# Two layers of a graph-attention kernel: two sets of sums and the keys' terms by DMA in layer 2, a two-piece f32r spread of them in layer 3

## The chip, the cores and the metric

One core of one Trainium2 chip runs the whole program. The metric is the device time of one execution in microseconds; lower is better. The engines are named as the profile names them: PE (matrix multiply; PEld its weight loads), DVE (vector), ACT (activations), POOL (GpSimd), and SP, whose queue issues nearly all DMAs.

## The reference

Four graph-attention layers run one after the other on 8 graphs of 1024 nodes and 128 features, each followed by a residual and a layer norm. Layers 0 and 1 are dot-product attention with four heads. Layers 2 and 3, which the change touches, score additively:

```python
# layer 2, one head of width 128            # layer 3, four heads of width 32
s_i = Wh @ a1                               # ei, ej per head
s_j = Wh @ a2
e = leaky_relu(s_i[:, :, None] + s_j[:, None, :], negative_slope=0.2)
e = where(mask, e, -inf)                    # layer 3: -9e15
attention = softmax(e, axis=-1)
h_prime = attention @ Wh                    # then elu
```

Here s_j is the "keys' term": one number per node j. To take the softmax stably, the kernel needs for each node i the largest s_j among its neighbours.

## The kernel before, in words

A **unit** is one graph and head: 8 units in layer 2, 32 in layer 3. A unit is worked in 16 **tiles** of 128 keys by 512 queries, numbered tt = 0 to 15: tiles 0 to 7 are the first half of the queries (c = 0), 8 to 15 the second (c = 1). A tile passes through the engines so:

- `scores` (PE, L1046 or L1051, then L1053): mask and query terms summed in one of four PSUM banks (0 to 3). For two tiles in four ACT has first written a relu there (L832).
- `settle` (DVE, L1382, the other two tiles in four) and `exps` (ACT, L858): the exponential.
- `take_low` (POOL, L329): reads two operands in SBUF and writes the low part of the f32 exponential as f16.
- `weigh` (PE, L1094): 20 matmuls of 129 columns (33 in layer 3) that add the tile into the sums, 6 tiles after its scores (`LAGS`).

After the last tile of a half DVE divides the sums (`half_done`, L1431 to L1437) and adds one to `s_accfree`. In layer 2 the sums of a half fill banks 6 and 7, and both halves use the same two; `weigh` at the first tile of a half waits on `s_accfree` until the half before is divided. In layer 3 a half needs one bank, and the two halves alternate between 6 and 7.

The largest neighbour is found ahead of time. `spread` (PE, L1003) multiplies a column of ones by the row of s_j, in plain f32 with one row, so that all 128 partitions of banks 4 and 5 hold the row. `take_max` (DVE, L1350, a custom instruction that adds the mask and takes the maximum) then runs 8 times per unit, over that PSUM row and `mask_n` in SBUF. Of unit U+2's maxima six are taken during unit U, after tiles 7, 9, 11, 13, 14 and 15 (`MAX_AFTER`), and the last two during unit U+1, after tiles 1 and 2 (`MAX_NEXT`). `spread` for unit U+2 is issued after the scores of tile 7 (`SPREAD_AT`). `find_shift` (DVE, L1330 to L1334) follows at tile 4, then SP's `place_shift` puts the result, in 8 small DMAs (L527), into the row that `scores` of the next unit reads.

All of it is written as one instruction stream per engine; every engine runs its stream in order and stops at each semaphore wait. SP's stream in each unit is `store_output`, `place_shift`, a wait for PE, `load_unit` for three units ahead (L494). Before the first tile of a layer, DVE takes all maxima of unit 0, finds its shift, and takes six of unit 1.

## Time and profile before

| what | us |
|---|---|
| median of 3 runs | 2969.57 (2963.59 to 2971.39) |
| the profiled execution | 2962.04 |
| its span | 2960.2 |
| layer 2, first scores to last `weigh` | 1729 to 2026 |
| layer 3, first `spread` to last `weigh` | 2184 to 2882 |

Over the span PE is busy 78%, DVE 73%, POOL 63%, ACT 54%. An engine's idle time is given in the profile with what ended it ("<-"); an engine that waits on a semaphore at the head of its queue is idle. "PEclk" is the granted TensorE clock as a share of 2.4 GHz; 0.50 is 1.2 GHz.

### The profile page before, as it was taken

The numbers are of one execution on the slowest core, as the hardware profiler recorded it, in microseconds if no ns is written. First come the engines' busy times: TensorE is split into PE (matmuls) and PEld (weight loads), VectorE is DVE, ScalarE is ACT, GpSimd is POOL, SyncE is SP. The second block draws the span as 40 slices with busy tenths as digits, with TensorE's granted clock in tenths as the row PEclk, the third lists the DMA queues.
The fourth block names the chain that finished last, engine by engine and source line by source line (L and its number), as shares of the span: only waits on it lengthen the run. The fifth ranks groups of instructions, "written<-read, shape, count | busy, mean of one in ns | idle before, by whom it ended". The sixth has DMA issues, their size and how long they took to land.

```text
span 2960.2 us, 89198 instructions
## 1 busy us (share of the span) xinstructions
PE 2309.2 (78%) x32745; PEld 1617.6 (55%) x33080; DVE 2157.0 (73%) x4078; ACT 1585.4 (54%) x2273; POOL 1853.8 (63%) x1837
## 2 busy tenths in 40 slices
PE   4588888887565999999957668884659988989980
PEld 3366666666442556666635446663426665666660
DVE  4499999999464999999933354433759988888965
ACT  3344444454363555555534534444727776777775
POOL 2288888888341778777853434443318877777873
PEclk9788888888676999999976679997769998898995
DMA  7922333331575222232235421102631211111117
GB/s 245 322 69 71 77 78 78 77 77 27 127 229 172 61 63 61 63 71 64 63 77 168 136 73 52 52 16 95 156 83 50 48 45 42 46 44 42 50 31 162
DMA packets 336189, 263.48 MB, mean 89 GB/s; under 512 B 229688, under 2 KB 293432, under 8 KB 335856
## 3 DMA queue, kind: packets, MB, share of 16 engines
q1 hardware_dynamic: 331248, 241.83, 30.7%
q0 software_dynamic: 4608, 16.78, 1.5%
q8 instruction: 262, 4.29, 0.6%
q14 instruction: 71, 0.58, 0.1%
HBM read 162.84 MB, written 95.36 MB: 87 GB/s over the span
## 4 chain that ended last, share of the span: by engine, by line
PE 45%; issue 17%; DVE 16%; ACT 7%; SPq 5%; DMA 4%; POOL 2%; DVEq 1%; ACTq 0%; POOLq 0%
PE ps L1094 15%; PE ps L1053 7%; DVE xn L1408 4%; SPq L527 4%; PE ps L1034 3%; PE ps L1003 3%; PE ps L941 3%; ACT xn L721 2%; DVE cv L1370 2%; DVE full L1350 2%; DMA qs<-nshift 2%; PE ps L1012 2%; PE ps L1038 2%; PE ps L965 2%; PE ps L1051 2%
## 5 line engine op out<-in xcount | busy, mean ns | idle before, releaser
L329 POOL TENSOR_TENSOR xc<-part 128x512 f16<-128x512 f32 x1536 | 1604.7, 1073 | 626.6 <-ACT part L858 473.1
L1094 PE MATMUL ps<-vs,part 128*128 128x33 bf16 (+1 forms) x13824 | 845.9, 188 | 46.2 <-DVEq L1443 44.5
L1094 PEld LDWEIGHTS ps<-vs,part 128*128 128x128 bf16 x13824 | 674.0, 101 | 352.9 <-issue 207.6
L1350 DVE CUSTOM_DVE_ANT_0 full<-ps,mask_n 128x1024 bf16<-128x1024 f32 x576 | 695.5, 1218 | 150.7 <-PE ps L1003 71.8
L1094 PE MATMUL ps<-vs,xc 128*128 128x33 bf16 (+1 forms) x9216 | 775.5, 186 | 9.5 <-issue 9.5
L1094 PEld LDWEIGHTS ps<-vs,xc 128*128 128x128 f16 x9216 | 593.9, 99 | 6.8 <-issue 6.8
L840 ACT ACTIVATE part<-cv,lift 128x1024 f32<-128x1024 f32 x256 | 294.8, 1152 | 321.5 <-DVE cv L1370 298.5
L858 ACT ACTIVATE part<-ps 128x512 f32<-128x512 f32 x512 | 305.6, 597 | 281.3 <-PE ps L1038 281.3
L1053 PE MATMUL ps<-qs,sel 128*128 128x512 f32 x640 | 416.0, 651 | 17.0 <-ACT ps L832 17.0
L1034 PE MATMUL ps<-qs,ks 128*128 128x512 f32 x512 | 287.9, 565 | 123.3 <-DVE cv L1370 91.4
L1382 DVE SCALAR_TENSOR_TENSOR cv<-ks,colx,ps 128x512 f32<-128x512 f32 x320 | 238.7, 746 | 182.9 <-PE ps L1053 145.9
L858 ACT ACTIVATE part<-cv,cols 128x512 f32<-128x512 f32 x320 | 229.7, 718 | 239.4 <-DVE cv L1382 233.3
L1370 DVE SCALAR_TENSOR_TENSOR cv<-ps,mask_t 128x1024 f32<-128x1024 f32 x256 | 311.8, 1219 | 43.9 <-PE ps L1034 20.3
L1038 PE MATMUL ps<-qs,ks 97*128 97x512 f32 x512 | 301.8, 590 | 3.1 <-DMA qs<-nshift 3.0
L858 ACT ACTIVATE part<-ps,colx 128x512 f32<-128x512 f32 x320 | 215.0, 672 | 81.0 <-PE ps L1053 75.9
L1076 PEld LDWEIGHTS ps<-vs,part 128*128 128x128 bf16 x2048 | 160.9, 98 | 133.2 <-issue 95.5
L1076 PE MATMUL ps<-vs,part 128*128 128x99 bf16 x2048 | 229.6, 212 | 1.0 <-POOL xc L329 1.0
L832 ACT ACTIVATE ps<-ks,colx 128x512 f32<-128x512 f32 x316 | 218.7, 692 | 11.4
L1078 PE MATMUL ps<-vs,xc 128*128 128x66 bf16 x2048 | 216.0, 194 | 0.0
L1012 PE MATMUL ps<-ks,qs 96*128 96x512 f32 x512 | 188.4, 451 | 21.1 <-DMA vs<-v_d 18.6
L1034 PEld LDWEIGHTS ps<-qs,ks 128*128 128x128 f32 x512 | 111.0, 218 | 132.5 <-DVE cv L1370 90.9
L1078 PEld LDWEIGHTS ps<-vs,xc 128*128 128x128 f16 x2048 | 168.6, 99 | 0.0
(145 smaller groups left out, 3313.7 us busy)
## 6 DMA issues: line engine op xcount, KB each, us to landing
qs<-q_d SPq DMA_DIRECT2D x224, 128.0 KB
ks<-k_d SPq DMA_DIRECT2D x224, 128.0 KB
ks<-row_d SPq DMA_DIRECT2D x40, 512.0 KB
vs<-v_d SPq DMA_DIRECT2D x96, 198.0 KB
q_d<-part SPq DMA_DIRECT2D x32, 512.0 KB
k_d<-part SPq DMA_DIRECT2D x32, 512.0 KB
ctx_d<-xn SPq DMA_DIRECT2D x96, 128.0 KB, 1.8
xc<-ctx_d SPq DMA_DIRECT2D x96, 128.0 KB, 4.4
```

Of the source, the lines that this page charges most:

```text
L329: eng.tensor_tensor(plo[:, r, :], prob[:, r, :], phi[:, r, :], ALU.subtract).then_inc(low_done(layer, u, s)[0], 1)
L840: act.activation(prob[:, r:r + 2, :], arg[:, a:a + 2, :], ACT.Exp, scale=2.0 * CLIP, bias=lift[:, 0:1]).then_inc(s_exp, 2)
L858: act.activation(prob[:, r, :], src, ACT.Exp, **more).then_inc(s_exp, 1)
L1012: mm = pe.matmul(ps[:, at + c, :], qs[0:96, n, k * P:(k + 1) * P], ks[0:96, n, c * HALF:(c + 1) * HALF], start=True, stop=True)
L1034: mm = pe.matmul(bank, ks[:, n, blk_j], qs[:, n, cut], start=True, stop=True)
L1038: mm = pe.matmul(bank, ks[0:97, n, blk_j], qs[0:97, n, cut], start=False, stop=True)
L1053: mm = pe.matmul(bank, sel[:, 2, :], qs[:, n, cut], start=False, stop=True, skip_group_check=True)
L1076: pe.matmul(ps[:, 6 + c, at_a:at_a + V3], phi[:, r, it * P:(it + 1) * P], vs[:, n, at_v:at_v + V3], start=opens, stop=False, skip_group_ch ...
L1078: mm = pe.matmul(ps[:, 6 + c, at_a:at_a + 66], plo[:, r, it * P:(it + 1) * P], vs[:, n, at_v:at_v + 66], start=False, stop=True, skip_grou ...
L1094: mm = pe.matmul(acc, half[:, r, it * P:(it + 1) * P], vs[:, n, at:at + width], start=opens and h == 0 and v == 0, stop=h == 1 and v == 1, ...
L1350: dve.tensor_tensor_reduce(junks[k % 2], src, mask_n[:, k, :], 1.0, least, ALU.add, ALU.max, accum_out=dst).then_inc(s_nmax, 1)
L1370: dve.scalar_tensor_tensor(arg[:, a:a + 2, :], ps[:, r:r + 2, :], -0.5, mask_t[:, j:j + 2, c * HALF:(c + 1) * HALF], ALU.max, ALU.min).the ...
```

## The change

In layer 2 the second half of the queries sums in banks 4 and 5, the first in 6 and 7, and `weigh` waits for the half before the last one. The keys' terms no longer pass through PE and PSUM there: SP copies the row of s_j from HBM to all 128 partitions of SBUF (`load_keys`, 512 KB), in turn into half of `full` and into `work`, and `take_max` reads it there. In layer 3 `spread` stays, but takes 0.2 s_j as two f32r pieces in two rows and multiplies by ones divided by 0.2; the second row costs one more load per unit. The two scratch rows of `take_max` now share one half of `full`.

```diff
-LOADS = (9, 7, 7, 8)
+LOADS = (9, 7, 6, 9)
-        junks = [full[:, k, :].bitcast(BF16)[:, 0:NODES] for k in range(2)]
+        junks = [full[:, 0, :].bitcast(BF16)[:, k * NODES:(k + 1) * NODES] for k in range(2)]
+        keys = [full[:, 1, :], work[:, :, :].rearrange("p t f -> p (t f)")]
...
-                    go(qs[32:33, n, :].bitcast(F32), row_d[0, bass.ds(r + heads, 1)])
+                    if layer == 3:
+                        for k in range(2):
+                            go(qs[32 + k:33 + k, n, :].bitcast(F32), row_d[2 + k, bass.ds(r + heads, 1)])
...
+            def load_keys(g, n):
+                sp.wait_ge(s_nmax, max_count(SHIFT0[2] + g - 1))
+                sp.dma_start(keys[n % 2], row_d[0, bass.ds(g * 8 + 1, 1)].to_broadcast([P, NODES])
+                             ).then_inc(s_keys[n % 2], 16)
...
+                if layer == 2:
+                    for n in range(2):
+                        load_keys(n, n)
...
+                        if layer == 2 and not (last and n >= UNROLL - 2):
+                            load_keys(g + 2, n)
...
-                        mm = pe.matmul(ps[:, 4 + c, :], sel[32:33, 1, :].bitcast(F32),
-                                       qs[32:33, n, c * HALF:(c + 1) * HALF].bitcast(F32), start=True, stop=True)
+                        mm = pe.matmul(ps[:, 4 + c, :], sel[32:34, 1, :], qs[32:34, n, c * HALF:(c + 1) * HALF],
+                                       start=True, stop=True)
...
-                            pe.wait_ge(s_accfree, H - (0 if layer == 2 else 1) - 2 * UNITS[0])
+                            pe.wait_ge(s_accfree, H - 1 - 2 * UNITS[0])
...
-                                acc = ps[:, 6 + it // 2, it % 2 * width:(it % 2 + 1) * width]
+                                acc = ps[:, 6 - 2 * c + it // 2, it % 2 * width:(it % 2 + 1) * width]
...
-                            if layer > 1 and one_after and tt == SPREAD_AT:
+                            if layer == 3 and one_after and tt == SPREAD_AT:
...
-            dve.memset(sel[32:34, 1, :].bitcast(F32), 1.0).then_inc(s_sel, 1)
+            dve.memset(sel[32:34, 1, :].bitcast(F32), 1.0 / SLOPE).then_inc(s_sel, 1)
...
+                        if layer == 2:
+                            src = keys[n % 2]
+                        if k == 0 and layer == 2:
+                            dve.wait_ge(s_keys[n % 2], u * (16 * (UNROLL // 2)) + (n // 2 + 1) * 16)
...
-                        banks = ((6, 2), (7, 2)) if layer == 2 else ((6 + c, IB),)
+                        banks = ((6 - 2 * c, 2), (7 - 2 * c, 2)) if layer == 2 else ((6 + c, IB),)
```

On PE, at tile 7 of layer 2's first unit (L1046 and L1053 are scores, L1003 the spread, L1094 `weigh`), before:

```order
L1046 MATMUL ps<-mask_t,ident_b 128x512 [waits s_relu]
L1053 MATMUL ps<-qs,sel 128x512
L1003 MATMUL ps<-qs,sel 128x512 [waits s_nmax,s_stk2]
L1003 MATMUL ps<-qs,sel 128x512
L1094 MATMUL ps<-vs,part 128x129 [waits s_lo]
L1094 MATMUL ps<-vs,part 128x129 x2
L1094 MATMUL ps<-vs,xc 128x129 x2
```

and in the changed kernel, where the same functions have other line numbers (L1063 and L1070 scores, L1111 `weigh`):

```order
L1063 MATMUL ps<-mask_t,ident_b 128x512 [waits s_relu]
L1070 MATMUL ps<-qs,sel 128x512
L1111 MATMUL ps<-vs,part 128x129 [waits s_lo]
L1111 MATMUL ps<-vs,part 128x129 x2
L1111 MATMUL ps<-vs,xc 128x129 x2
```

The spread and its two waits are gone from between scores and `weigh`. On DVE, from the end of `find_shift` at tile 4 to tile 9 of a layer 2 unit ("ISA full,top" is `take_max`, "ISA top" the read of its result), before:

```order
L1334 SCALAR_TENSOR_TENSOR colx<-cols 128x8
L1382 SCALAR_TENSOR_TENSOR cv<-ks,colx,ps 128x512 [waits s_exp,s_score,s_colx]
L1350 ISA full,top<-ps,mask_n 128x1024 [waits s_nmax,s_nsc]
L1350 ISA top 128x1
L1382 SCALAR_TENSOR_TENSOR cv<-ks,colx,ps 128x512 [waits s_exp,s_score]
L1350 ISA full,top<-ps,mask_n 128x1024 [waits s_nmax]
```

and now:

```order
L1350 SCALAR_TENSOR_TENSOR colx<-cols 128x8
L1402 SCALAR_TENSOR_TENSOR cv<-ks,colx,ps 128x512 [waits s_exp,s_score,s_colx]
L1370 ISA full,top<-full,mask_n 128x1024 [waits s_nmax,s_keys0]
L1370 ISA top 128x1
L1402 SCALAR_TENSOR_TENSOR cv<-ks,colx,ps 128x512 [waits s_exp,s_score]
L1370 ISA full,top<-full,mask_n 128x1024 [waits s_nmax]
```

The order is the same; the first operand of `take_max` moves from PSUM (ps) to SBUF (full, in the next unit work), and the wait from PE's s_nsc to the DMA's s_keys0. On SP's queue, the third unit's loads and what follows ahead of layer 2's first tile, before:

```order
L494 DMA qs<-row_d 1x1024
L494 DMA ks<-row_d 128x1024
L494 DMA qs<-row_d 1x1024 x2
L494 DMA cols<-col_d 128x8 x2
L494 DMA vs<-v2_d 128x3096
L527 DMA qs<-nshift 1x128x1 [waits s_shcol]
L527 DMA qs<-nshift 1x128x1 x7
```

and now:

```order
L497 DMA ks<-row_d 128x1024
L497 DMA qs<-row_d 1x1024 x2
L497 DMA cols<-col_d 128x8 x2
L497 DMA vs<-v2_d 128x3096
L539 DMA full<-row_d 128x1024 [waits s_nmax]
L539 DMA work<-row_d 128x1024 [waits s_nmax]
L533 DMA qs<-nshift 1x128x1 [waits s_shcol]
L533 DMA qs<-nshift 1x128x1 x7
```

The first two key rows are queued behind the loads of three units.

## Rows read from the trace of the kernel before

**Rows 1.** Windows: length, busy us (instructions) by engine, PEclk, DMA share, GB/s

```profile
1808.20:1845.70 37.50, 31.32 (x355) 25.00 (x358) 18.58 (x41) 16.79 (x25) 16.38 (x16) 0.91 0.17 51
...
2402.10:2421.60 19.50, 18.41 (x378) 12.81 (x383) 18.05 (x36) 15.53 (x25) 16.09 (x17) 1.00 0.20 49
2334.80:2354.90 20.10, 19.30 (x376) 13.21 (x382) 18.31 (x35) 15.55 (x25) 16.12 (x17) 0.92 0.21 48
2354.90:2380.70 25.80, 20.79 (x351) 13.59 (x357) 18.42 (x36) 15.96 (x26) 17.22 (x17) 0.74 0.16 39
```

**Rows 2.** Waits, layer 2 (1730 to 2030): who waited for whom, total, times, longest

```profile
PE ps L1094 <- DVEq L1443: 44.5, 15, 3.6
```

**Rows 3.** Timeline of PE in layer 2: start, length, instruction, [idle before]

```profile
1813.07 0.51 PE L1094 MATMUL ps<-vs,part 128*128 128x129 bf16 x3 [2.55 <-DVEq L1443]
...
1815.28 0.99 PE L1053 MATMUL ps<-qs,sel 128*128 128x512 f32 x1
1816.20 2.01 PE L1003 MATMUL ps<-qs,sel 1*128 1x512 f32 x4
1818.14 0.35 PE L1094 MATMUL ps<-vs,part 128*128 128x129 bf16 x3
...
1819.34 0.58 PE L1053 MATMUL ps<-qs,sel 128*128 128x512 f32 x1
1819.77 0.35 PE L1094 MATMUL ps<-vs,part 128*128 128x129 bf16 x3
...
1820.97 0.58 PE L1053 MATMUL ps<-qs,sel 128*128 128x512 f32 x1
```

**Rows 4.** Groups by line, layer 2: count, busy us, mean ns, idle before

```profile
L329 POOL TENSOR_TENSOR xc<-part 128x512 f16<-128x512 f32 x128 | 131.0, 1040 | 189.6 <-ACT part L858 153.6 <-issue 36.0
...
L1350 DVE CUSTOM_DVE_ANT_0 full<-ps,mask_n 128x1024 bf16<-128x1024 f32 x54 | 65.6, 1219 | 31.4 <-PE ps L1003 29.6 <-DVE xn L1437 1.8
L1382 DVE SCALAR_TENSOR_TENSOR cv<-ks,colx,ps 128x512 f32<-128x512 f32 x64 | 47.8, 747 | 114.7 <-PE ps L1053 94.0 <-issue 20.5
```

**Rows 5.** Timeline of POOL and DVE in layer 1's node stage

```profile
801.08 2.33 POOL L640 TENSOR_TENSOR vs<-xc,rows 128x1024 f32<-128x1024 f32 x1
...
802.06 2.44 DVE L1251 TENSOR_TENSOR full<-full,rows 128x1024 f32<-128x1024 f32 x1 [3.44 <-ACT full L721]
```

**Rows 6.** DVE lines with all operands in SBUF: ns min/median/max

```profile
L1251 DVE TENSOR_TENSOR full<-full,rows x8: 1224/2439/2446, 767.4 to 900.9; 128x1024 f32<-128x1024 f32 x8
```

```profile
L329 DVE TENSOR_TENSOR xc<-part x128: 685/1015/1573, 968.5 to 1516.0; 128x512 f16<-128x512 f32 x128
```

```profile
L1331 DVE SCALAR_TENSOR_TENSOR nshift<-shift x40: 166/961/966, 1722.6 to 2849.1; 128x8 f32<-128x8 f32 x40
```

**Rows 7.** Timeline ahead of layer 2's first tile

```profile
1709.02 3.75 PE L1003 MATMUL ps<-qs,sel 1*128 1x512 f32 x4 [16.56 <-DMA vs<-v_d]
...
1713.08 1.23 DVE L1350 CUSTOM_DVE_ANT_0 full<-ps,mask_n 128x1024 bf16<-128x1024 f32 x1 [17.58 <-PE ps L1003]
...
1726.51 1.22 DVE L1350 CUSTOM_DVE_ANT_0 full<-ps,mask_n 128x1024 bf16<-128x1024 f32 x1 [3.56 <-PE ps L1003]
```

**Rows 8.** One window there, columns as in Rows 1

```profile
1714.00:1716.00 2.00, 0.00 (x0) 0.00 (x0) 2.00 (x5) 0.00 (x0) 0.00 (x0) 0.50 0.46 186
```

**Rows 9.** Timeline of PE in layer 3

```profile
2403.06 1.98 PE L1003 MATMUL ps<-qs,sel 1*128 1x512 f32 x4
2404.97 0.24 PE L1094 MATMUL ps<-vs,part 128*128 128x33 bf16 x3
```

**Rows 10.** Windows of 1 us in layer 3, columns as in Rows 1

```profile
2340.00:2341.00 1.00, 1.00 (x22) 0.83 (x22) 1.00 (x4) 0.09 (x1) 0.69 (x1) 0.50 0.17 17
```

**Rows 11.** Waits, layer 3 (2230 to 2882)

```profile
DVE cv L1382 <- PE ps L1053: 50.4, 49, 3.2
```

**Rows 12.** Timeline ahead of layer 3's first tile

```profile
2201.48 1.22 DVE L1350 CUSTOM_DVE_ANT_0 full<-ps,mask_n 128x1024 bf16<-128x1024 f32 x1 [3.55 <-PE ps L1003]
```

**Rows 13.** Window in layer 2's node stage, columns as in Rows 1

```profile
1600.00:1660.00 60.00, 46.96 (x237) 35.31 (x235) 23.00 (x69) 32.61 (x52) 28.76 (x40) 0.68 0.63 190
```

More of the change, by code:

```diff
@@ L223, in build @@
         s_relu = sem("s_relu")
+        s_keys = [sem("s_keys0"), sem("s_keys1")]
         s_open = sem("s_open")
@@ L1131, in heads @@
                         unit_ready(n, 0)
-                        if layer > 1:
+                        if layer == 3:
                             spread(n, U + n)
-                            continue
-                        for k in range(BLOCKS if n == 0 else len(MAX_AFTER[1])):
+                        for k in range((BLOCKS if n == 0 else len(MAX_AFTER[1])) if layer == 1 else 0):
                             top_scores(n, k, U + n)
@@ L1336, in find_shift, with take_max @@
                     dve.wait_ge(s_colx, U - SHIFT0[2] + 1)
-                def take_max(k, U, n):
+                def take_max(k, U, n, u=0):
                     dve.wait_ge(s_nmax, max_count(U) + k - 1)
@@ L1346, in take_max @@
                         src, least, dst = pf[:, 4 * HALF:6 * HALF], LOWEST, top[:, k, 0:1]
-                        if k == 0:
-                            dve.wait_ge(s_nsc, BLOCKS * SHIFT0[2] + U - SHIFT0[2] + 1)
+                        if layer == 2:
+                            src = keys[n % 2]
+                        if k == 0 and layer == 2:
+                            dve.wait_ge(s_keys[n % 2], u * (16 * (UNROLL // 2)) + (n // 2 + 1) * 16)
+                        elif k == 0:
+                            dve.wait_ge(s_nsc, BLOCKS * SHIFT0[2] + U - SHIFT0[3] + 1)
                     dve.sem_inc(s_carry, 1)
@@ L1461, in body @@
                             if tt in MAX_NEXT[layer] and next_one:
-                                take_max(MAX_NEXT[layer][tt], U + 1, n + 1)
+                                take_max(MAX_NEXT[layer][tt], U + 1, n + 1, u)
                             if layer > 1 and tt == FIND_AT and next_one:
@@ L1465, in body @@
                             if tt in MAX_AFTER[layer] and one_after:
-                                take_max(MAX_AFTER[layer][tt], U + 2, n + 2)
+                                take_max(MAX_AFTER[layer][tt], U + 2, n + 2, u)
                         e = s - lag - 1
```

## The prediction, made before the changed kernel ran

> **What bounds the kernel now.** I read the windows of one unit in each layer first, then the waits of layer 2, then the timelines of PE and DVE where the waits stood. A layer 2 unit takes 37.5 us. PE is busy for 31.3 of them, DVE for 18.6, ACT for 16.8, POOL for 16.4 [rows 1]: PE sets the pace there and is itself stopped for some 6 us. In 15 places `weigh` waits for DVE to divide the half before, 44.5 us in all [rows 2]. The timeline shows one: 2.55 us idle at 1813.07, and after it the score matmul at 1815.28 takes 0.99 us instead of 0.58, because the granted clock stands at its lower level, 1.2 GHz, until PE has worked a while. Then comes the spread, from 1816.20 to 1818.14, 1.94 us; and then tiles that follow each other by 1820.97 - 1819.34 = 1.63 us [rows 3].
>
> Layer 3 is another case. A unit whose clock stays at 2.4 GHz takes 19.5 us, with PE busy 18.4 and DVE 18.05; one with a stretch at 1.2 GHz takes 20.1 [rows 1]. In the first kind DVE is the bound: its 1.4 idle microseconds are short gaps between its own dependent instructions. So PE time there is worth less than its length.
>
> **The change, part by part.** The sum is made against the profiled execution, 2962.04 us (span 2960.2); the median of the runs is 2969.57, 7.5 above it.
>
> *Two sets of sums.* The wait for the half before becomes a wait for the one before that, which DVE divided 8 tiles (13 us) earlier. All 44.5 us of idle go [rows 2]. So does what they cost in clock: of the 37.5 us of a unit, 16 tiles of 1.63 are 26.1, two stops (44.5/15 each) 5.9, the spread 1.9; the 3.6 left over are two restarts at the lower clock, 1.8 each, 15 of them 27 us.
>
> *No spread in layer 2.* Six spreads lie between tiles (units 2 to 7), 6 x 1.94 = 11.6 us of PE [rows 3]. Together 83 us, if nothing else takes PE's place; a unit would then take 26.1 us.
>
> *Maxima from SBUF.* This is the price. Before, `take_max` reads one operand from PSUM and takes 1219 ns at any time [rows 4]. Now both lie in SBUF, and POOL's `take_low`, 16 a unit of 1040 ns [rows 4], also reads SBUF. What that does is seen elsewhere in the trace. In layer 1's node stage POOL's L640 runs from 801.08 to 803.41; DVE's L1251, both operands in SBUF, starts at 802.06 and ends at 804.50, which is POOL's end plus 1.1 us [rows 5]. Alone it takes 1224 ns, beside POOL 2439; L329 on DVE 685 alone, 1015 in the middle, 1573 at most; even the 8-element L1331 goes from 166 to 961 [rows 6]. So a DVE instruction with two SBUF operands waits for POOL's current one to end, up to 1.04 us, and POOL waits for it in turn. The Trainium skill says the same (SBUF — State Buffer, "Who interferes with whom": two SBUF inputs on DVE contend with a GpSimd instruction that reads SBUF, and the loser is blocked for the whole instruction). By that rule, the trace agrees, and it speaks against this part of the change.
>
> How much: POOL's 16 x 1.04 = 16.6 and DVE's 8 x 1.22 = 9.8 come to 26.4 us of exclusive use in a unit that PE wants to do in 26.1. If every max waits a full `take_low`, DVE needs 18.6 + 8 x 1.04 = 26.9, and some 1.6 more for two slowed instructions of `find_shift`: 28.5 us, 2.4 above PE, 19 us over 8 units. If no max waits, nothing. The 6 tiles between scores and `weigh` (9.8 us, against about 3.1 for one tile's way through settle, exp and low) absorb much, but five maxima fall on tiles 13 to 18, where DVE falls behind. I take 1.5 us a unit, nearer the upper end, 12 us.
>
> *Start of layer 2.* Before, DVE's first max is at 1713.08, after a spread of 3.75 us at the lower clock that began when unit 0's loads were there; later DVE stands 3.56 us until the second spread is done [rows 7]. Now the first key row is queued behind three units' loads, of which the last arrive about 1715: in 1714 to 1716 the DMA engines are busy 0.46 of the time at 186 GB/s, so 404 GB/s when they work [rows 8]. 0.5 MB at that rate are 1.3 us more, and with about a microsecond to land it is there near 1717. That is 4 us later, and 3.6 come back because unit 1's maxima no longer wait. I book nothing; if the rows land together with the very last load it is 3 to 5 us worse. The wait of `load_keys` on SP is for maxima taken long ago, and the copy is issued about a unit ahead of its use, so nothing behind it on SP's queue (`store_output`, `place_shift`) is held up; the 4 MB in total lie in a queue that is busy 17% of a unit [rows 1].
>
> Layer 2: 83 - 12 = 71 us.
>
> *The f32r spread in layer 3.* Before, four passes and 1.91 us (2403.06 to 2404.97) [rows 9]. The scores of a tile are also two matmuls of 512 columns, one bf16 and one f32r; from their start, 1819.34, to the next `weigh`, 1819.77, pass 0.43 us [rows 3]. So I take 0.43 for the two f32r matmuls of the new spread, and 0.87 at 1.2 GHz. No row shows one with two rows. PE saves 1.5 us a unit. With DVE as the bound only these parts count:
> - Ahead of the first tile both spreads lie on the chain, at 3.75 us each (the row in [rows 7] is layer 2's, layer 3's two are as long, and the second again holds DVE for 3.55 [rows 12]): 2 x 2.9 = 5.8 us.
> - Nineteen units of 20.1 us hold about 3.4 us at 1.2 GHz (a microsecond of it is in [rows 10]), in which PE loses 1.7 us. With 1.5 us less work PE no longer holds DVE up, and the unit goes to DVE's 19.4 to 19.5: 19 x 0.65 = 12 us. DVE's waits for PE's scores, 50.4 us in the layer [rows 11], bound this and the next item from above.
> - Eight units go slower for other reasons (five of about 26 us, in which PE stands still for 5 us where the loop turns, [rows 1] has one, and three of 21 to 22 behind it). There PE leads, mostly at the lower clock, and I take 1.1 us each, 9 us.
>
> Layer 3: 27 us. Its extra load of 4 KB a unit on SP lies behind `place_shift` and costs nothing; if SP were late it would show as PE waiting for nshift.
>
> **Sum:** 2962.0 - 71 - 27 = 2864. The runs lie somewhat above the profiled one; I forecast 2867.
>
> **The rivals.**
> *A, the forecast:* PE stays the bound of layer 2 at 27 to 28 us a unit, DVE of layer 3.
> *B, the port between DVE and POOL decides layer 2:* in the dense stretch settle, exp and low come so late that PE stops again and restarts at 1.2 GHz. For it: 26.4 us of exclusive use in 26.1. Against it: 9.8 us of slack per tile, and ACT is free a third of the time. At 33 us a unit, which is 28.5 and two stops with restart of 2.2 each, layer 2 gains 83 - 8 x 6.9 = 28 us: 2910.
> *C, PE's saving counts in full in layer 3:* 30 x 1.5 + 5.8 = 51 us there instead of 27, and 2840. Against it: DVE's 18.05 busy microseconds with their gaps make the 19.5 that the fast units take now [rows 1].
> *D, slower: the clock in layer 3.* PE gets 2.5 to 3 idle us a unit, and the level falls when it idles: in the node stage ahead of layer 2 PE is busy 78% of the time and the mean clock is 0.68 [rows 13]. PE needs 18.4 - 1.5 = 16.9 us a unit at full clock; at a mean of 0.87 it would match DVE, and to eat layer 2's 71 us over 32 units the unit must reach 20.2 + 2.2 = 22.4 us, a mean clock of 0.75. Worked out at 0.72, 23.5 us a unit: 2891 + 32 x 3.3 = 2997. Against it: a PE that is waited for does not idle, so the loss limits itself.
> *E, no change:* only if PE's waits were replaced one for one, say by the key rows landing late for every unit. They are asked for a unit ahead.
>
> **How the numbers follow.** A 0.68, B 0.18, C 0.08, D 0.03, E 0.03. A's own range is from 2848 (no lock cost, and layer 3 with 31) to 2885 (lock cost 19, layer 3 only 17, start 5 worse, then the runs' scatter). To leave out 2 in 10 at most, the range runs to B: 2842 to 2910. A measurement here tells from no change what is over 0.3% (9 us). Faster 0.94, same 0.02, slower 0.04.
>
> **What would show it.** Layer 2: no PE wait on `half_done`, units of 27 to 28 us, clock near 1.0 within them, 8 maxima a unit with a median between 1.3 and 2.2 us, and POOL's `take_low` with a tail above 1.04. Layer 3: spread 0.43 us, units near 19.5, DVE hardly ever waiting for scores. The first max of layer 2 near 1717 on the old scale. I am wrong if the maxima stay at 1.22 (then 2855), if layer 2 units exceed 30 us (B), or if layer 3 units stay at 20.1 in spite of the shorter spread, which would mean that the lower clock, not the spread, sets them.

## The result, and the profile after

| what | before | changed | forecast |
|---|---|---|---|
| median, us | 2970.48 (2963.59 to 2991.56, 4 runs) | 2841.65 (2835.98 to 2847.84, 4 runs) | 2867 |
| span of the profiled execution | 2960.2 | 2834.1 | 2862 |
| layer 2, first to last `take_low` | 283.6 | 200.3 | 283.6 - 71 = 212.6 |
| layer 3, first to last `take_low` | 668.3 | 626.9 | 668.3 - 21 = 647.3 |

The ratio is 0.9555, 95% interval 0.9503 to 0.9607: 129 us faster where 103 were forecast. The time lies 0.35 us below the range (2842 to 2910) and 6 below the forecast's own (2848 to 2885). In the profiled executions layer 2 gave 12 us more than was forecast and layer 3 gave 20 us more. Ahead of them the changed kernel is 3.5 us later (last `take_low` of layer 1 at 1519.9, before 1516.4); from there to layer 2's first tile nothing changed (219.0 us, before 218.6), as booked.

The spans of the two layers are read from POOL's instructions: duration in ns (min/median/max), then first and last start. Before:

```profile
L329 POOL TENSOR_TENSOR xc<-part x128: 1038/1040/1050, 1735.0 to 2018.6; 128x512 f16<-128x512 f32 x128
L329 POOL TENSOR_TENSOR xc<-part x512: 1036/1040/1070, 2209.9 to 2878.2; 128x512 f16<-128x512 f32 x171
```

and in the changed kernel, with the maxima of layer 2 (L1370):

```profile
L332 POOL TENSOR_TENSOR xc<-part x128: 1034/1042/2114, 1738.9 to 1939.2; 128x512 f16<-128x512 f32 x128
L332 POOL TENSOR_TENSOR xc<-part x512: 1032/1042/1073, 2126.1 to 2753.0; 128x512 f16<-128x512 f32 x171
L1370 DVE CUSTOM_DVE_ANT_0 full<-work,mask_n x25: 1211/1389/1953, 1739.7 to 1892.7; 128x1024 bf16<-128x1024 f32 x25
L1370 DVE CUSTOM_DVE_ANT_0 full<-full,mask_n x24: 1212/1390/2086, 1744.8 to 1867.0; 128x1024 bf16<-128x1024 f32 x24
```

The contention is there: maxima of up to 2.09 us instead of 1.22 [rows 4], `take_low` of up to 2.11. The windows (columns as in [rows 1]: length, PE, PEld, DVE, ACT, POOL, PEclk, DMA share, GB/s) show what became of it. One unit of layer 2, then of layer 3 an ordinary unit, one at the loop's turn, the one behind it, and the first:

```profile
1817.30:1844.10 26.80, 26.80 (x363) 22.45 (x361) 22.46 (x42) 17.06 (x26) 21.35 (x18) 1.00 0.29 91
...
2306.80:2326.40 19.60, 17.59 (x384) 12.65 (x384) 18.11 (x37) 15.63 (x26) 16.22 (x17) 1.00 0.21 49
2425.80:2448.90 23.10, 18.51 (x370) 12.94 (x370) 18.62 (x36) 16.14 (x26) 17.11 (x17) 0.85 0.16 43
2448.90:2467.40 18.50, 17.92 (x396) 12.90 (x393) 16.41 (x35) 15.03 (x24) 15.18 (x16) 1.00 0.21 52
2129.20:2147.10 17.90, 16.80 (x359) 12.03 (x360) 17.43 (x33) 15.43 (x25) 16.07 (x17) 1.00 0.21 47
```

In layer 2 PE is busy for the whole unit at 2.4 GHz, where it was busy for 31.3 of 37.5 us at a mean clock of 0.91 [rows 1]; DVE's busy time went from 18.6 to 22.5 us and POOL's from 16.4 to 21.4, both still below 26.8. The six units between start and end of the layer take 23.9 to 26.8 us, 25.7 in the mean. No PE wait on the divided half is left (it was [rows 2]); DVE's wait for scores in layer 3 halved, from [rows 11] to:

```profile
DVE cv L1402 <- PE ps L1070: 26.5, 26, 2.9
```

The new spread on PE in layer 3, to be compared with the old one in [rows 9]:

```profile
2307.31 0.58 PE L1070 MATMUL ps<-qs,sel 128*128 128x512 f32 x1
2307.82 0.73 PE L1020 MATMUL ps<-qs,sel 2*128 2x512 f32 x2
2308.48 0.24 PE L1111 MATMUL ps<-vs,part 128*128 128x33 bf16 x3
```

From its start to the next `weigh` pass 0.66 us, before 1.91. The saving is 1.25 us; the forecast was a spread of 0.43 us and a saving of 1.5.

The units of layer 3, in us (means), as the 30 periods from unit 1's to unit 31's between the starts of the second instruction of `find_shift` (L1331 before, L1347 now). Counted from its first instruction, a unit at a turn is 0.3 to 0.6 us shorter and the one behind it 0.4 to 0.7 longer; their sum stays.

| | first | 19 ordinary | 5 at a turn | 5 behind a turn |
|---|---|---|---|---|
| before | 22.5 | 19.95 | 26.1 | 20.8 |
| changed | 17.9 | 19.4 | 22.8 | 19.0 |
| gain in sum | 4.6 | 11 | 16.5 | 9 |

The ordinary units did what was forecast (12 us). The other eleven gave 30 us; 9 were booked for them. The experiments had two questions: why does the contention in layer 2 cost nothing, and where do the 30 us come from.

### The profile page after: what moved, and what is told of

It reads as the page before. It is cut to its first block, busy times and chain, and to the rows that moved or that the text cites. A ratio compares the mean times of both kernels' runs of the same rounds, so it can differ in the third digit from the quotient of the medians.

```text
span 2834.1 us, 89438 instructions
## 1 busy us (share of the span) xinstructions
PE 2200.2 (78%) x32984; PEld 1571.2 (55%) x32984; DVE 2176.8 (77%) x4078; ACT 1577.9 (56%) x2273; POOL 1882.5 (66%) x1837
## 4 chain that ended last, share of the span: by engine, by line
PE 37%; issue 18%; DVE 18%; ACT 8%; SPq 7%; DMA 5%; POOL 2%; DVEq 1%; ACTq 0%; POOLq 0%
PE ps L1111 12%; SPq L533 5%; DVE xn L1428 4%; PE ps L1070 4%; DMA qs<-nshift 3%; PE ps L958 3%; ACT xn L738 3%; DVE full L1370 3%; DVE cv L1390 2%; PE ps L1051 2%; PE ps L1063 2%; PE ps L1068 2%; PE ps L1029 2%; PE ps L982 2%; PE ps L1054 2%
## 5 line engine op out<-in xcount | busy, mean ns | idle before, releaser
L332 POOL TENSOR_TENSOR xc<-part 128x512 f16<-128x512 f32 x1536 | 1633.0, 1094 | 473.6 <-ACT part L875 326.3
L1111 PE MATMUL ps<-vs,part 128*128 128x33 bf16 (+1 forms) x13824 | 823.5, 186 | 1.2 <-DVE work L1419 1.1
L1111 PEld LDWEIGHTS ps<-vs,part 128*128 128x128 bf16 x13824 | 658.5, 99 | 272.0 <-issue 202.7
L1111 PE MATMUL ps<-vs,xc 128*128 128x33 bf16 (+1 forms) x9216 | 762.1, 184 | 4.4 <-issue 4.4
L1370 DVE CUSTOM_DVE_ANT_0 full<-ps,mask_n 128x1024 bf16<-128x1024 f32 x512 | 618.4, 1218 | 88.5 <-DVE xn L1462 29.0
L1111 PEld LDWEIGHTS ps<-vs,xc 128*128 128x128 f16 x9216 | 583.2, 97 | 0.1
L1070 PE MATMUL ps<-qs,sel 128*128 128x512 f32 x640 | 380.1, 596 | 0.0
L1093 PEld LDWEIGHTS ps<-vs,part 128*128 128x128 bf16 x2048 | 161.0, 98 | 133.1 <-issue 96.3
L849 ACT ACTIVATE ps<-ks,colx 128x512 f32<-128x512 f32 x316 | 218.7, 692 | 11.5
L1054 PE MATMUL ps<-mask_t,ident_b 128*128 128x512 bf16 x512 | 198.2, 387 | 16.2 <-DMA qs<-nshift 10.4
L1029 PE MATMUL ps<-ks,qs 96*128 96x512 f32 x512 | 188.5, 451 | 21.7 <-DMA vs<-v_d 19.2
```

The costliest lines, as they stand in the source:

```text
L332: eng.tensor_tensor(plo[:, r, :], prob[:, r, :], phi[:, r, :], ALU.subtract).then_inc(low_done(layer, u, s)[0], 1)
L1029: mm = pe.matmul(ps[:, at + c, :], qs[0:96, n, k * P:(k + 1) * P], ks[0:96, n, c * HALF:(c + 1) * HALF], start=True, stop=True)
L1054: pe.matmul(bank, ident_b[:, :], mask_t[:, j, cut], start=True, stop=False)
L1070: mm = pe.matmul(bank, sel[:, 2, :], qs[:, n, cut], start=False, stop=True, skip_group_check=True)
L1093: pe.matmul(ps[:, 6 + c, at_a:at_a + V3], phi[:, r, it * P:(it + 1) * P], vs[:, n, at_v:at_v + V3], start=opens, stop=False, skip_group_ch ...
L1111: mm = pe.matmul(acc, half[:, r, it * P:(it + 1) * P], vs[:, n, at:at + width], start=opens and h == 0 and v == 0, stop=h == 1 and v == 1, ...
```

## The experiments

Each kernel is compared with the kernel before on the same chip; "layer 3" below is the time between its first and last `take_low`.

### The parts alone

e1 is the kernel before with the f32r spread in layer 3 only:

```diff
-LOADS = (9, 7, 7, 8)
+LOADS = (9, 7, 7, 9)
...
+                        if layer == 3:
+                            mm = pe.matmul(ps[:, 4 + c, :], sel[32:34, 0, :], qs[32:34, n, c * HALF:(c + 1) * HALF],
+                                           start=True, stop=True)
+                            continue
...
+            dve.memset(sel[32:34, 0, :].bitcast(F32), 1.0 / SLOPE).then_inc(s_sel, 1)
```

> Layer 3's two-piece spread alone, layer 2 as before. Theory 1 (the parts add): layer 3 takes what it takes in the changed kernel, from first to last take_low 627 us against 668 before, plus 4 us ahead of it; the whole kernel is 45 us faster than before, about 2925 against 2970. Theory 2 (layer 3 was helped by what layer 2 left behind, such as where loads land): less than 30 us. My prediction's sum said 27 us.

Measured: 2926.65 us, ratio 0.9875 (0.9853 to 0.9897), 37 us faster. Layer 3 takes 635.6 us, 32.7 less, and layer 2 283.6 as before. An ordinary unit:

```profile
2390.20:2409.70 19.50, 17.49 (x381) 12.54 (x381) 18.05 (x35) 15.53 (x25) 16.11 (x17) 1.00 0.19 50
```

e2 is the changed kernel with the old spread in layer 3:

```diff
-LOADS = (9, 7, 6, 9)
+LOADS = (9, 7, 6, 8)
...
-                        mm = pe.matmul(ps[:, 4 + c, :], sel[32:34, 1, :], qs[32:34, n, c * HALF:(c + 1) * HALF],
-                                       start=True, stop=True)
+                        mm = pe.matmul(ps[:, 4 + c, :], sel[32:33, 1, :].bitcast(F32),
+                                       qs[32:33, n, c * HALF:(c + 1) * HALF].bitcast(F32), start=True, stop=True)
...
-            dve.memset(sel[32:34, 1, :].bitcast(F32), 1.0 / SLOPE).then_inc(s_sel, 1)
+            dve.memset(sel[32:34, 1, :].bitcast(F32), 1.0).then_inc(s_sel, 1)
```

> Layer 2's part alone, layer 3 with the plain f32 spread. Theory 1 (the parts add): layer 2 takes 200 us from first to last take_low against 284 before, layer 3 668 as before, whole kernel about 83 us faster, 2887. Theory 2: layer 3 gets shorter than 660 without any change of its own.

Measured: 2877.83 us, ratio 0.9715 (0.9692 to 0.9737), 86 us faster. The parts add up, 37 + 86 = 123 of 129 us. Against e2 the changed kernel saves 35.4 us between layer 3's first and last tile (662.3 to 626.9): first unit 4.2, 19 ordinary ones 12, five at a turn 11.5 (25.1 to 22.8 each), five behind 8 (20.6 to 19.0). So the spread is most of what works at the turn. Layer 2's part gives layer 3 another 6 to 9 us though it changes nothing in layer 3's own code: 668.3 to 662.3 without the new spread (e2 against the kernel before), 635.6 to 626.9 with it (the changed kernel against e1), most of it at the turns.

e3 keeps the keys' DMA but gives layer 2 back its single set of sums:

```diff
-                            pe.wait_ge(s_accfree, H - 1 - 2 * UNITS[0])
+                            pe.wait_ge(s_accfree, H - (0 if layer == 2 else 1) - 2 * UNITS[0])
...
-                                acc = ps[:, 6 - 2 * c + it // 2, it % 2 * width:(it % 2 + 1) * width]
+                                acc = ps[:, 6 + it // 2, it % 2 * width:(it % 2 + 1) * width]
...
-                        banks = ((6 - 2 * c, 2), (7 - 2 * c, 2)) if layer == 2 else ((6 + c, IB),)
+                        banks = ((6, 2), (7, 2)) if layer == 2 else ((6 + c, IB),)
```

> The changed kernel with one set of sums in layer 2, as before; the keys still come by DMA and are read in SBUF. Theory 1 (the stops on half_done are most of layer 2's gain, 44.5 us of idle and 27 us at the lower clock): layer 2 is about 70 us longer than in the changed kernel, 270 us from first to last take_low, and PE waits for half_done 15 times again, about 45 us. Theory 2 (the spread's removal did more than its 12 us): layer 2 below 255 us.

Measured: 2910.6 us, ratio 0.9821 (0.9801 to 0.9841). Layer 2 takes 272.4 us: the missing spread gives 11.2, which is the 11.6 forecast for it, and the second set of sums 72.1 (272.4 to 200.3), which is 44.5 + 27 = 71.5. The waits are back as they were [rows 2]:

```profile
PE ps L1111 <- DVEq L1463: 44.9, 15, 4.1
```

### The contention in layer 2

e8 replaces POOL's `take_low` in layer 2 by a memset, which reads nothing; the low part is left out of layer 2's sums.

```diff
+            if layer == 2:
+                eng.memset(plo[:, r, :], 0.0).then_inc(low_done(layer, u, s)[0], 1)
+                return
```

> The changed kernel with POOL's take_low of layer 2 replaced by a memset of the same tile: the low part of the exponential is left out and POOL reads nothing there. If the lock between DVE's two SBUF operands and POOL's reads is what lengthens layer 2's maxima (1286 ns in the middle, 2086 at most), all become 1.22 us. If layer 2 is bound by PE, its time stays within 3 us of the changed kernel's 200; if the lock still costs what I booked (12 us), it drops by that.

Measured: 2844.73 us, one run. The maxima are back at 1.22 us, every one:

```profile
L1373 DVE CUSTOM_DVE_ANT_0 full<-work,mask_n x30: 1216/1218/1228, 1739.6 to 1899.2; 128x1024 bf16<-128x1024 f32 x30
...
1798.40:1824.50 26.10, 26.10 (x352) 21.99 (x355) 18.39 (x43) 16.49 (x25) 8.38 (x16) 1.00 0.29 93
```

DVE is busy for 18.4 us again and POOL for 8.4, yet PE still fills the unit, with 16 tiles of 1.63 us. The six units from the second shift to the eighth take 153.4 us, in the changed kernel 154.0, and the layer 200.1 against 200.3. The contention is real and costs under 1 us in the whole layer, not 12.

### The two rows at the head of layer 2

e9 queues each of the two first key rows ahead of the loads of its own unit:

```diff
+                    if layer == 2 and n < 2:
+                        load_keys(n, n)
                     load_unit(layer, 0, n)
```

> The changed kernel with each of the first two key rows loaded ahead of its unit's other loads. In the changed kernel the first max of layer 2 stands at 1719.9 us, 7 us later than before. If the queue behind three units' loads is the cause, the first max starts about 10 us earlier and the whole kernel is 6 to 10 us faster than the changed one, near 2833. If other loads of unit 0 are what DVE waits for, under 3 us.

Measured: 2832.25 us, ratio 0.9553 (0.9532 to 0.9573); by the ratios, which scatter by several us, it can't be told from the changed kernel's 0.9555. The traces can tell them apart. The first max starts 191.9 us after layer 1's last `take_low`; in the changed kernel it is 200.0, before 196.7. In the changed kernel this is the wait and what the DMA engines do just ahead of it, busy all the time at 411 GB/s:

```profile
1719.93 1.23 DVE L1370 CUSTOM_DVE_ANT_0 full<-full,mask_n 128x1024 bf16<-128x1024 f32 x1 [21.89 <-DMA full<-row_d]
...
1717.00:1719.00 2.00, 0.00 (x0) 0.00 (x0) 0.00 (x0) 0.00 (x0) 0.00 (x0) 0.50 1.00 411
```

From layer 1's last `take_low` to layer 2's first pass 210.8 us, in the changed kernel 219.0; in e12 and e13, which have the same edit, 212.4 and 212.3, and in all eleven kernels with the key rows queued last 218.2 to 220.6. The place in the queue costs 8 us, and undoing it gives them.

### What bounds an ordinary unit of layer 3

e6 takes layer 3's maxima over the first 512 keys only, which takes work from DVE and none from PE:

```diff
+                    w = HALF if layer == 3 else NODES
```

> The changed kernel with layer 3's maxima taken over the first 512 keys alone (the other 512 are left out of the maximum), which takes about 4.3 us of DVE time off each unit. If DVE is the bound of layer 3 now, its units go from 19.5 us to PE's 17.6 or a little below; if PE is, they stay at 19.5.

Measured: 2794.41 us, one run; layer 3 590.6. An ordinary unit goes to 18.0 us in the mean, and PE nearly fills it. One of them:

```profile
2307.10:2324.90 17.80, 17.65 (x403) 13.02 (x405) 14.48 (x35) 15.51 (x25) 16.02 (x17) 1.00 0.22 54
```

So DVE was the bound at 19.4 us. A unit at a turn still takes 22.6 us, with a stop of PE of 3.5 to 4.4 us.

### The lower clock

e4 and e5 make the spread of the changed kernel a little longer than the old one, with seven more matmuls of 512 columns ahead of each of the 32 spreads. In e4 they are two-row f32r ones like the spread, in e5 bf16 ones over all 128 rows. At the full clock the padded spread then takes 2.28 us (median 2.29 in e4, 2.28 in e5) up to the next `weigh`, the old one 1.91.

```diff
+                    for k in range(7):
+                        pe.matmul(ps[:, 4, :], sel[32:34, 1, :], qs[32:34, n, 0:HALF], start=True, stop=True)
```

```diff
+                    for k in range(7):
+                        pe.matmul(ps[:, 4, :], ident_b[:, :], mask_t[:, 0, 0:HALF], start=True, stop=True)
```

> The changed kernel with 7 idle f32r matmuls of two rows ahead of each spread of layer 3, so that a spread costs PE about 1.9 us again, as in plain f32. Theory 1 (layer 3's gain is PE time where PE leads): layer 3 goes back to about 668 us from first to last take_low, 40 more than the changed kernel. Theory 2 (the plain f32 form itself did the harm, by other means than its length): it stays near 627.

> The same with 7 bf16 matmuls of 128 rows as the padding, also about 1.5 us. Theory 1 (PE time alone): the same layer 3 time as with the two-row padding, within 5 us, and the same stretches at 1.2 GHz. Theory 3 (the granted clock fell because of what PE did in the spread, one row, not because of its length): the stretches at 1.2 GHz inside the units are gone, units take 19.4 to 19.6 us, layer 3 is 15 us or more shorter than with the two-row padding.

Measured: e4 2901.57 us, ratio 0.9764 (0.9718 to 0.9811); e5 2870.11, ratio 0.9665 (0.962 to 0.9709). An ordinary unit, one at a turn and the one behind it, in e4:

```profile
2351.50:2371.90 20.40, 19.63 (x382) 14.12 (x386) 18.28 (x35) 15.75 (x25) 16.18 (x17) 0.92 0.19 47
2371.90:2399.60 27.70, 21.18 (x377) 14.76 (x382) 19.04 (x35) 16.69 (x26) 17.27 (x17) 0.75 0.15 36
2399.60:2420.70 21.10, 20.36 (x393) 14.55 (x396) 16.72 (x37) 15.17 (x25) 15.35 (x16) 0.92 0.19 46
```

and in e5:

```profile
2333.10:2352.60 19.50, 17.77 (x368) 12.46 (x373) 18.10 (x36) 15.64 (x26) 16.18 (x17) 1.00 0.21 49
2352.60:2379.80 27.20, 20.86 (x370) 13.84 (x373) 18.36 (x35) 15.95 (x26) 17.09 (x17) 0.81 0.15 37
2379.80:2400.40 20.60, 19.86 (x418) 14.03 (x423) 16.54 (x36) 15.61 (x25) 15.23 (x16) 1.00 0.20 48
```

Both give PE the same number of matmuls of the same columns, for the same time. With two-row f32r ones the granted clock falls to the lower level in every unit (mean 0.917 in ordinary ones, which take 20.5 us); with full-row bf16 ones it stays at 1.00 in 18 of the 19 and the unit at DVE's 19.5. Layer 3 takes 682.0 us in e4 and 654.6 in e5: 27 us are the clock alone. The two paddings differ in rows and in type, and no run separates these; that f32r alone does not do it is argued from the changed kernel, whose scores are f32r over 128 rows and whose ordinary units are all at 1.00. But e5 is still 27.7 us above the changed kernel, and nearly all of it is in the first unit (1.7), at the turns (26.6 against 22.8 us) and behind them (20.0 against 19.0).

### The turn: load traffic

At the turn SP issues the loads of a unit just as PE stops. e10 puts them off by twelve tiles in the changed kernel, e11 in the kernel before:

```diff
-                            sp.wait_ge(s_av, CREDIT + TILES * UNIT0[layer] + g * TILES)
+                            late = TILES - 4 if layer == 3 and n == UNROLL - 1 else 0
+                            sp.wait_ge(s_av, CREDIT + TILES * UNIT0[layer] + g * TILES + late)
```

> The changed kernel; in layer 3 the fourth unit's loads of each loop body are held back until PE has done two tiles of the next body, so that no load runs while PE turns the loop. In the kernels so far PE stands 3.3 to 3.6 us at the turn where the copy of 512 KB is issued 0.1 to 0.6 us before PE gets there, and 4 to 5 us, mostly with a second stop of 1.1 to 1.4, where it is issued 1 to 2 us before. Theory A (PE's stop at the turn is made longer by load traffic that is in flight): all five stops get shorter than 3.3 us and alike, layer 3 shrinks by up to 10 us. Theory B (the stop is PE's own and its length comes from what PE did before): they stay at 3.3 to 3.6 and the time stays.

> The same deferral in the kernel before, nothing else. Theory A: the five stops of 3.6 to 5.0 us and the five second ones of 1.1 to 1.7 fall to what the deferred changed kernel has, the five long units go from 26 to about 22 us, layer 3 from 668 to about 650. Theory B: they stay at 26, and the time at 2965 to 2970.

Measured: e10 2841.58 us, ratio 0.9563 (0.9517 to 0.961), layer 3 624.4; e11 2962.39, ratio 0.9983 (0.9962 to 1.0004), layer 3 662.0. The profiled execution of e10 is the fastest of its four by 10 us, so its 624.4 says little; PE's stops in it are 3.2 to 3.5 us (changed kernel 3.3 to 5.0). In e11 the first stop shrinks to 3.3 to 3.75 us from 3.6 to 5.0, but the second one, in `weigh` some 3 us later, grows from 1.1 to 1.7 us to 1.6 to 1.9, and the two together only go from 5.5 to 5.3 us in the mean:

```profile
2461.98 0.39 PE L1052 MATMUL ps<-mask_t,ident_b 128*128 128x512 bf16 x1 [3.75 <-issue]
2464.54 0.22 PE L1095 MATMUL ps<-vs,xc 128*128 128x33 bf16 x2 [1.56 <-issue]
```

The traffic explains up to 1.5 us of a first stop, and not the difference between the kernels.

### The turn: instructions, time or place

The idle time before these matmuls waits on no semaphore ("issue"). Seven padding matmuls change PE's time and the number of its instructions at once. e14 and e15 add two and seven matmuls of 33 columns ahead of each of the 32 spreads, 64 and 224 in all (the first expectation below counts e14's too high). Two bring the number of matmuls that the trace records to that of the old spread, which counts as four [rows 9]. This is e15; e14 has `range(2)`:

```diff
+                    for k in range(7):
+                        pe.matmul(ps[:, 4, 0:33], ident_b[:, :], mask_t[:, 0, 0:33], start=True, stop=True)
```

e16 runs 28 of them once, ahead of layer 3's loop, which moves only the place of the loop's body in PE's program. Theory F says that the number of instructions in the body makes the stop long, theory T that PE's time does, and the third that the body's place does.

> The changed kernel with two small full-row bf16 matmuls of 33 columns ahead of each spread, in layer 3 only (64 spreads, 128 matmuls). They add instructions to PE's loop body and next to no time. Open is why PE stops at layer 3's loop turn for 3.3 to 3.6 us in the changed kernel and for 3.6 to 5.0 us, and then once more for 1.1 to 1.7 us, in the kernel before (and 4.2 to 5.2 and 1.1 to 1.4 in the two kernels with seven padding matmuls for each spread). Theory F, the stop grows with the number of instructions in the loop's body: it becomes longer than 3.6 us or its second part comes back, the five units at a turn go from 22.8 to 24 us or more, and layer 3 from 627 to some 635. Theory T, the stop follows from PE's time, as how far PE is ahead of or behind the other engines when it comes to the turn: stops of 3.3 to 3.6 us with no second part, turn units of 22 to 23.5 us, layer 3 within 3 us of 627.

> The changed kernel with seven small full-row bf16 matmuls of 33 columns ahead of each spread, in layer 3 only: as many instructions as the kernel with seven 512-column ones, but less than a fifth of their time. Theory F, number of instructions: stops as there, 4.8 to 5.2 us and then 1.1 to 1.4, turn units near 26.5 us, units behind a turn near 20, layer 3 near 650. Theory T, PE's time: stops of 3.3 to 3.6 us with no second part, turn units of 22 to 24 us, layer 3 under 635.

> The changed kernel with 28 small matmuls of 33 columns run once, ahead of layer 3's loop: the loop's body keeps its length and only its place in PE's program moves. Theory F and theory T both: stops of 3.3 to 3.6 us, layer 3 within 3 us of 627. A third theory, that the stop depends on where the body lies in the program and not on its length: stops change here, to over 4 us or with a second part.

Measured: e14 2840.03 us, ratio 0.9558 (0.9529 to 0.9587); e15 2852.79, 0.9601 (0.9573 to 0.9629); e16 2839.64, 0.9556 (0.9519 to 0.9594). The mean units, PE's stops at the turn and, in the last column, how many 16 KB packets the DMA queue "instruction" (q8) moves between two turns:

| kernel | layer 3 | at a turn | behind | ordinary | first stop | second stop | q8 |
|---|---|---|---|---|---|---|---|
| before | 668.3 | 26.1 | 20.8 | 19.95 | 3.6 to 5.0 | 1.1 to 1.7 | 15 |
| e2, old spread | 662.3 | 25.1 | 20.6 | 20.0 | 4.4 to 6.0 | none | 15 |
| e11, deferral | 662.0 | 24.9 | 21.1 | 19.9 | 3.3 to 3.75 | 1.6 to 1.9 | 15 |
| e4, seven of 2x512 | 682.0 | 27.2 | 20.9 | 20.5 | 4.2 to 5.1 | 1.1 to 1.4 | 15 |
| e5, seven of 128x512 | 654.6 | 26.6 | 20.0 | 19.5 | 4.75 to 5.2 | 1.1 to 1.4 | 15 |
| e15, seven of 128x33 | 639.6 | 25.0 | 18.7 | 19.5 | 3.3 to 4.8 | 1.1 to 2.4 | 15 |
| e1, old layer 2 | 635.6 | 23.8 | 19.2 | 19.4 | 3.4 to 4.75 | 1.1, at two turns | 14 |
| e16, place | 634.0 | 23.8 | 19.4 | 19.4 | 3.8 to 5.1 | none | 14 |
| e14, two of 128x33 | 628.0 | 22.9 | 19.0 | 19.4 | 3.3 to 4.7 | none | 14 |
| changed | 626.9 | 22.8 | 19.0 | 19.4 | 3.3 to 5.0 | none | 14 |

In e15 the second stop is back although PE's time hardly changed (0.93 us for the spread with its padding up to the next `weigh`, 0.66 without):

```profile
2364.15 0.39 PE L1070 MATMUL ps<-mask_t,ident_b 128*128 128x512 bf16 x1 [3.54 <-issue]
2367.17 0.21 PE L1113 MATMUL ps<-vs,xc 128*128 128x33 bf16 x1 [1.83 <-issue]
```

Neither theory F nor T holds alone. More instructions bring the second stop and 12.7 us of layer 3 (e15 against the changed kernel), but two more per unit, as many as the old spread had, cost 1.1 us, within the scatter. PE's time alone, from e15 to e5, costs 15.0 us and all of it where PE had to stop or start: 1.7 in the first unit, 1.65 at each turn, 1.3 behind each, nothing in ordinary units. For the 0.27 us of e15 that rate gives 15.0 x 0.27 / 1.35 = 3 us, an estimate.

That the place of the body costs time is not shown. The profiled execution of e16 has a layer 3 of 634.0 us, where six kernels with PE's code in and ahead of layer 3 as it is in the changed kernel, or as long (the changed one, e3, e8, e9, e10, e12), have 624.4 to 628.5. But it is the slower of e16's two runs (2842.87 and 2836.41), and its median, 2839.64, is not above the changed kernel's 2841.65.

### The turn: what the instruction queue does

The traces hold one thing more. The DMA queue that the profile calls "instruction" (q8) moves packets of 16 KB, one every 6 us or so in layer 3; the records don't say for which engine. In all 17 kernels, at all five turns, such a packet starts while PE stands still, 0.4 to 2.5 us after the stop has begun. In 82 of these 85 stops PE goes on 2.7 to 3.2 us after the packet's start; in the other three, all of e2, the packet itself takes 1.8 to 2.1 us, where most take about 1, and PE goes on after 3.8 to 4.4. Between two turns, from 2371.5 to 2458.5 in the kernel before and from 2360.7 to 2441.0 in the changed one, the queue's line (packets, MB, share) is:

```profile
q8 instruction: 15, 0.25, 1.2%
q8 instruction: 14, 0.23, 1.1%
```

The last column above has this count for each kernel. Seven small matmuls a unit add the fifteenth packet, two don't. Of the six kernels with 15 packets five have a second stop at every turn, and it ends 2.2 to 3.1 us after the start of the next packet; the sixth, e2, has the longest first stops. Of the eleven with 14 only e1 has one, at two turns. And with the loads deferred (e10 to e13) the packet starts 0.4 to 1.0 us into the stop at all 20 turns, without that up to 2.5. So the stops go with the times of these packets, a body that needs one more mostly stops once more, and with the loads deferred the packet comes earlier. This is read from the packets' times in the traces; no run was made to test it.

### Versions built on these

e12 is the changed kernel with the edits of e9 and e10. e13 adds one more: the three products of `find_shift` (L1348 to L1350), eight elements each, become one instruction with a constant tile, since DVE bounds layer 3.

```diff
-                    dve.scalar_tensor_tensor(colx[:, n, 0, :], col, SLOPE, col, ALU.mult, ALU.subtract)
...
+                    dve.tensor_tensor(colx[:, n, :, :], times[:, :, :], col.unsqueeze(1).to_broadcast([P, 3, BLOCKS]),
+                                      ALU.mult).then_inc(s_colx, 1)
```

> Key rows first and the deferral together. If both hold: the first max about 8 us earlier relative to the end of layer 1 than in the changed kernel, and layer 3 as with the deferral alone; about 2825 us, or 2832 if the deferral gives nothing.

> As the one before, and find_shift's three small products of the column become one DVE instruction with a constant tile (the factors -0.8, 0.8 and 0.2 in one product each, rounded otherwise). In layer 3 the three take 0.15, 1.00 and 0.15 us, the 1.00 being a wait for POOL. If DVE is the bound of layer 3: units go from 19.45 to about 18.5 to 19.0, layer 3 is 15 to 30 us shorter. If PE or ACT is: under 5 us.

Measured: e12 2834.46 us, ratio 0.9536 (0.949 to 0.9583), which can't be told from e9. e13 2805.61, ratio 0.9433 (0.9385 to 0.9482), the fastest version that computes everything. Its ordinary unit is 1 us shorter, 18.4 us, and layer 3 takes 599.4, in e12 628.0:

```profile
2294.50:2313.00 18.50, 17.25 (x375) 12.47 (x381) 17.07 (x33) 15.51 (x25) 16.08 (x17) 1.00 0.21 52
```

## Why the prediction was right, and where it was wrong

**Two sets of sums, no spread in layer 2: right.** 44.5 + 27 us were booked for the sums and e3 shows 72.1; 11.6 for the spreads and e3 shows 11.2. Together 83.3 us, 83 booked. The 3.6 us a unit that no instruction accounted for were the restarts at the lower clock, as the prediction read them.

**Maxima from SBUF: the mechanism right, the size wrong.** Maxima and `take_low` block each other (1.39 us in the median and up to 2.09). The step that failed is "I take 1.5 us a unit, nearer the upper end, 12 us": measured under 1 in the whole layer (e8). The rule of the Trainium skill that the prediction cites (SBUF — State Buffer, "Who interferes with whom") agrees with both traces, contention with a reading POOL and none with a writing one, but it gives a price to the instruction, not to the kernel. The sum of exclusive use, 26.4 us in 26.1, made it look dear; but a wait of DVE costs only when tiles come late to PE, and DVE, at 22.5 busy us with the waits in them, stayed 3.6 below the 26.1 of PE's sixteen tiles. This is 12 of the 33 us that both layers gave beyond the forecast.

**Start of layer 2: right in sum.** First max 3.3 us later, and the old wait for the second spread gone; measured 0.4 us in all. What the prediction took for fixed, the place in the queue, was worth 8 us (e9).

**The spread ahead of layer 3: right.** 5.8 booked; from layer 2's last `take_low` to layer 3's first it went from 191.3 to 186.9 us, 4.4.

**Ordinary units of layer 3: right.** 19.4 us with DVE as the bound (e6), 11 of 12 us. The prediction had them all at 20.1; four of the nineteen were at full clock already, and the mean was 19.95. That PE's lower clock went with the old spread is shown by e1, where it is gone from every ordinary unit, and that it is not a matter of PE's time by e4 against e5. The new spread takes 0.66 us and not 0.43, which costs nothing there.

**The other units: wrong, and by most.** The step is "Eight units go slower for other reasons [...] There PE leads, mostly at the lower clock, and I take 1.1 us each, 9 us". Measured 30 us, of which the spread alone gives 24 (e2 against the changed kernel). Two errors lie in it.

- The count. Eleven units have PE on the path, not eight: the first one, five at a turn and all five behind them.
- The size. PE time saved there counts in the turn and once more behind it: 1.35 us of matmuls (a padded spread of 2.28 us in e5, 0.93 in e15) cost 1.65 + 1.3 us there, and 15.0 us over the layer. The lower clock adds 1.1 in the first unit, 0.5 at a turn and 0.9 behind it (e4 against e5, 8 us in the eleven).

An estimate from the two for the 1.25 us that the new spread saves is 15.0 x 1.25 / 1.35 + 8 = 22, near the 24. The remaining 6 us (e2 against the kernel before) come with layer 2's part of the change. Their cause is not shown; e16, the one kernel that changed PE's code ahead of layer 3 alone, left the median where it was.

**The sum.** On the scale of the profiled execution the forecast was 2864 and the measurement 2835.98, 28 us less: 33 from the two layers, less 3.5 by which the layers before them were slower and 1.4 ahead of layer 3. The forecast of the median then added 3 us where its own runs before lay 7.5 above the profiled one; the changed kernel's lie 5.7 above. "A's own range", 2848 to 2885, was worked out around 2864, so around 2867 it would be 2851 to 2888. That the time fell just outside the range, by 0.35 us, is chance, since single runs lie on both sides of its end; that it fell far below the forecast is not.

**The rivals.** C, the saving in full in layer 3, came nearest to the time (2840), but for another reason: ordinary units kept DVE's 19.4, and the time came from the turns and from layer 2's missing price. B had its mechanism in the trace and not its cost. D fails: the clock is 1.00 in every ordinary unit.

**Open.** Why PE stops at the turn was not tested. No semaphore releases it. The packets of the instruction queue fit all 85 stops, the second stops and what the deferral does; they leave open for which engine a packet is, and why a packet comes late without the deferral.

## What to carry to other kernels

Where two engines block each other, add the blocking to the busy time of each and compare it with the unit of the engine that sets the pace; below that it costs nothing, even when the sum of exclusive use reaches the unit. Where an engine is not the bound, ask in which units it still is (the first one, a loop's turn, the unit behind), count these, and price its saving there in full, twice where a late start is handed to the next unit (1.65 and 1.3 us for 1.35 us of matmuls, e5 against e15). And once an engine is shown to be the bound, its small instructions are next: three of eight elements made one were worth about 1 us in each ordinary unit (e13). A difference of a few us in one profiled layer needs the medians of the runs beside it: e16's 7 us did not stand there.

## What the runs showed of the hardware

- Seven matmuls of 512 columns over two rows in f32r go with a lower granted clock than as many over 128 rows in bf16, at the same duration: mean 0.917 against 0.996 in ordinary units, 27 us over layer 3 (e4, e5).
- In the padding at full clock f32r matmuls of 512 columns over two rows follow each other every 0.23 us (e4), bf16 ones over 128 rows every 0.22 (e5). Two two-row ones by themselves take 0.66 up to the next `weigh`.
- PE stands still for 3.2 to 6.0 us at the loop's turn in every kernel. In 82 of 85 such stops it goes on 2.7 to 3.2 us after a 16 KB packet of the instruction queue has started. Kernels with 15 such packets between two turns instead of 14 stop a second time for 1.1 to 2.4 us, except e2; of those with 14 only e1 does, at two turns.
- A DVE maximum with two SBUF operands of 1.22 us takes up to 2.09 beside a POOL that reads SBUF, and 1.22 beside one that only writes it (e8).
